# Attention with a quantised linear layer on one core: the prologue's products in another order, with half 1's queries last

## What is computed

```python
ct_q, ct_kv = x @ Wd_q + b, x @ Wd_kv + b            # 256 -> 128
query = (ct_q @ Wu_q + b) + rope(ct_q @ Wq_r + b)     # 128 -> 256
key   = (ct_kv @ Wu_k + b) + rope(x @ Wk_r + b)
value = ct_kv @ Wu_v + b
attn  = softmax(query_h @ key_h.T / sqrt(272))        # each head, 4096 x 4096
x = layernorm(x + concat_h(attn @ value_h) @ Wo + b)
x_int8 = clip(round(x / (max|x| / 127)), -128, 127)
x = layernorm(x + (x_int8 @ weight_int8.T) * x_scale * weight_scale.T + bias)
```

## Time and profile before

| | us |
|---|---|
| median of 3 runs | 1985.05 (1983.85 to 1987.11) |
| time of the profiled execution | 1983.67 |
| its span, first to last instruction | 1981.9 |
| ACT busy | 1815.3 (92% of the span) |
| PE busy | 1851.2 (93%) |
| DVE busy | 1582.6 (80%) |
| POOL busy | 163.4 (8%) |

### The profile page before, as it was taken

The page is one execution under the profiler, slowest core; times in us unless marked ns, Lnnn a source line. Parts: engine busy times, 40 slices in busy tenths (PEclk is TensorE's granted clock), DMA queues, the critical chain, the costliest instruction groups (busy, mean ns, idle before and its releaser), DMA issues.

```text
span 1981.9 us, 31796 instructions
## 1 busy us (share of the span) xinstructions
PE 1851.2 (93%) x13009; PEld 451.9 (23%) x13009; DVE 1582.6 (80%) x1500; ACT 1815.3 (92%) x2026; POOL 163.4 (8%) x134
## 2 busy tenths in 40 slices
PE   8967999999999999999999999999999999999955
PEld 3441112122121221221222222222122122222134
DVE  3653888888888888888888887888988898888458
ACT  4447999999999999999999999999999999999935
POOL 5723500000000000000000000000000300000012
PEclk9998999999999999999999999999999999999987
DMA  5644111101111111111121000111111101101012
GB/s 165 216 161 174 25 25 25 25 20 19 21 20 22 25 25 25 25 25 25 25 67 25 17 17 17 25 25 25 25 25 25 23 19 19 21 18 24 1 44 85
DMA packets 165483, 81.48 MB, mean 41 GB/s; under 512 B 130204, under 2 KB 146716, under 8 KB 164856
## 3 DMA queue, kind: packets, MB, share of 16 engines
q1 hardware_dynamic: 164024, 78.11, 15.3%
q10 hardware_dynamic: 1312, 1.32, 0.2%
HBM read 48.83 MB, written 29.23 MB: 39 GB/s over the span
## 4 chain that ended last, share of the span: by engine, by line
ACT 69%; PE 10%; issue 9%; DVE 6%; DMA 2%; POOL 2%; SPq 1%; ACTq 0%; DVEq 0%; POOLq 0%
ACT arena L800 55%; ACT parts_or_sums L800 14%; PE PS L601 5%; PE PS L558 3%; PE PS L640 1%; DVE arena L860 1%; PE PS L1044 1%; POOL arena L1363 1%; DVE bn L728 1%; DMA Qst<-parts_or_sums 1%; DMA arena<-arena 1%; POOL arena L1362 1%; DVE arena L1654 1%; POOL arena L1365 0%; DMA arena<-head_out 0%
## 5 line engine op out<-in xcount | busy, mean ns | idle before, releaser
L800 ACT ACTIVATE arena<-PS 128x1024 f32<-128x1024 f32 x1488 | 1396.5, 1134 | 31.4 <-PE PS L558 31.0
L601 PE MATMUL PS<-arena,Vh 128*32 128x512 f32 x6704 | 1082.6, 606 | 5.5 <-DVE arena L860 3.6
L558 PE MATMUL PS<-Qst,Kst 49*128 49x512 f16 x4096 | 710.7, 384 | 61.4 <-ACT arena L800 38.2
L860 DVE SCALAR_TENSOR_TENSOR arena<-arena 128x2048 f32<-128x2048 f32 x282 | 646.4, 2292 | 0.1
L836 DVE TENSOR_SCALAR arena<-PS 128x512 int32<-128x512 f32 x376 | 259.6, 690 | 269.4 <-PE PS L558 265.5
L558 PEld LDWEIGHTS PS<-Qst,Kst 49*128 49x128 f16 x4096 | 182.3, 93 | 1048.9 <-ACT arena L800 797.6
L601 PE MATMUL PS<-parts_or_sums,Vh 128*32 128x512 f32 x1488 | 386.0, 604 | 0.0
L800 ACT ACTIVATE parts_or_sums<-PS 128x1024 f32<-128x1024 f32 x372 | 369.3, 1137 | 2.8 <-PE PS L558 2.8
L601 PEld LDWEIGHTS PS<-arena,Vh 128*32 128x32 f32 x6704 | 155.9, 108 | 278.6 <-issue 270.0
L856 DVE SCALAR_TENSOR_TENSOR arena<-arena 128x2048 f32<-128x2048 f32 x94 | 216.0, 2297 | 0.0
L844 DVE TENSOR_SCALAR arena<-arena 128x2048 int32<-128x2048 int32 x94 | 115.7, 1230 | 7.3
(11 more groups left out here) (115 smaller groups left out, 606.6 us busy)
## 6 DMA issues: line engine op xcount, KB each, us to landing
Kst<-k_halves SPq DMA_DIRECT2D x64, 128.0 KB
Qst<-q_halves SPq DMA_DIRECT2D x64, 128.0 KB
Vh<-head_values SPq DMA_DIRECT2D x30, 256.0 KB, 4.4
arena<-xT_dram SPq DMA_DIRECT2D x8, 512.0 KB, 5.2
k_halves<-parts_or_sums SPq DMA_DIRECT2D x16, 256.0 KB, 2.4
k_whole<-arena SPq DMA_DIRECT2D x8, 512.0 KB, 3.3
q_halves<-parts_or_sums SPq DMA_DIRECT2D x16, 256.0 KB, 3.2
q_whole<-arena SPq DMA_DIRECT2D x8, 512.0 KB, 4.4
```

The lines of the kernel that those rows point to most:

```text
L558: return nc.tensor.matmul(out, Kst[par][low:low + HK + 1, at:at + 128], Qst[par][low:low + HK + 1, j * CH:(j + 1) * CH], start=True, stop= ...
L601: last = nc.tensor.matmul(bank(value_bank(t))[32 * j:32 * j + 32, :], Vh[t % 2][:, kt, :], moving, start=kt == first, stop=kt == last_kt)
L800: nc.scalar.activation(ring(at, k), bank(g % SLOTS * SLOT, k), ACT.Exp, scale=EXP_SCALE).then_inc(a.exp, 1)
L860: last = nc.vector.scalar_tensor_tensor(out=t, in0=t, scalar=POLY[3 - j], in1=power if j == 3 else mantissa, op0=ALU.add, op1=ALU.mult)
```

## The change

All products stand in one list, `PRODUCTS`, from which the programs of PE and ACT are written out without loops.

- Chunks 0 to 3 are made as before, keys and queries, eight products each. Then come the keys alone of chunks 4 to 7, then the queries alone of chunks 4 to 7, then the 16 groups of values. In the late parts the first product of chunk c+1 (`DKV` or `DQ_`) stands ahead of the last ones of chunk c.
- x and the tables of chunks 4 to 7 are loaded a second time for the late queries: `LOADS` has 12 entries, and a load's parity picks its buffer.
- DVE adds the two query weights of the upper 128 features once, so `QHI` is one matmul and not two: 13 per chunk and not 14. PE waits for this sum (`s_sum`).
- The lengths go into strips: each call writes four strips of 32 partitions of one bank, so that maxima and square roots read 128 partitions of 512 columns. The largest key length is brought to all partitions by a transpose and a matmul of one column. The calls stand between the late products.
- PE waits for the constants (`s_const`) ahead of its first product, where it waited after its last.
- On SP the stack of the first head (`load_stack`) stands between the loads of the late queries, the second stack after the stores of the last queries; shift rows come by way of DRAM.

```diff
+def make_products():
+    order = [("p", c, e) for c in range(HALF_CH) for e in range(8)]
+    late = range(HALF_CH, NCH)
+    order.append(("p", HALF_CH, DKV))
+    for c in late:
+        order += [("p", c, KR_)] + [("p", c + 1, DKV)] * (c + 1 < NCH) + [("p", c, UK_), ("p", c, KHI)]
+    order.append(("p", HALF_CH, DQ_))
+    for c in late:
+        order += [("p", c + 1, DQ_)] * (c + 1 < NCH) + [("p", c, QR_), ("p", c, UQ_), ("p", c, QHI)]
+    return order + [("v", 0, n) for n in range(KT // 2)]
...
+LOADS = list(range(NCH)) + list(range(HALF_CH, NCH))
...
+            def next_load(load, last_product, last_part):
+                if load + 2 < len(LOADS):
+                    sp.wait_ge(s_mm, DONE[last_product])
+                    load_x(LOADS[load + 2], load % 2)
+                    sp.wait_ge(s_rope, ROTATED[last_part])
+                    load_tables(LOADS[load + 2], load % 2)
...
+            for c in range(HALF_CH):
+                next_load(c, ("p", c, KHI), (c, "q"))
+                for n in "kq":
+                    store_parts(c, n)
+                    store_whole(c, n)
+            for c in range(HALF_CH, NCH):
+                next_load(c, ("p", c, KHI), (c, "k"))
+                store_parts(c, "k")
+                store_whole(c, "k")
+            next_load(NCH, ("p", HALF_CH, DQ_), (HALF_CH, "q"))
             for par in range(2):
-                load_stack(sp, fast.stack[par], par, par)
-            sp.wait_ge(s_shift, 1)
+                sp.wait_ge(s_parts["k"][par], 32 * HALF_CH)
+                sp.wait_ge(s_parts["q"][par], 32 * (HALF_CH // 2))
+            load_stack(sp, fast.stack[0], 0, 0)
+            next_load(NCH + 1, ("p", HALF_CH + 1, DQ_), (HALF_CH + 1, "q"))
+            for c in range(HALF_CH, NCH - 1):
+                store_parts(c, "q")
+                store_whole(c, "q")
+            store_shift(0)
+            store_parts(NCH - 1, "q")
+            store_whole(NCH - 1, "q")
+            sp.wait_ge(s_m, 16 * HALF_CH)
+            load_shift(sp, fast.stack[0], 0, 0)
+            load_stack(sp, fast.stack[1], 1, 1)
+            load_shift(sp, fast.stack[1], 1, 1)
+            store_shift(1)
...
-                    project(7, 7, [wcut(W_QR, lo=128), wcut(W_UQ, lo=128)], [cq, cq])
+                    QHI: ([wcut(W_UQ, lo=128)], [cq]),
...
             pe.wait_ge(s_const, 1)
-            pe.wait_ge(s_ev, E0 - 4)
+            for p in PRODUCTS:
+                if p == ("p", HALF_CH + 3, QR_):
+                    pe.wait_ge(s_ev, in_bank(SMALL_BANK))
+                    pe.wait_ge(s_kmax, 3)
+                    nc.tensor.transpose(PS[0:1, SMALL_BANK * CH:SMALL_BANK * CH + 128], kmax[:, 2:3], ident[:, :]).then_inc(s_kt, 1)
...
+                if p == ("v", 0, 13):
+                    lengths("q", 1, Q_LENGTH_BANKS[1])
+                product(p)
...
+            for p in PRODUCTS:
+                evacuate(p)
...
+                if p == ("v", 0, 2):
+                    shifts(0)
+                if p == ("v", 0, 14):
+                    shifts(1)
```

415 lines of the change are left out of this document (221 added, 194 removed).

## The result

| | before | after |
|---|---|---|
| median, us | 1985.31 (4 runs, 1983.85 to 1987.11) | 2007.03 (4 runs, 2006.57 to 2009.91) |
| ratio, 95% interval | | 1.0112 (1.0099 to 1.0125) |
| profiled execution: time, span | 1983.67, 1981.9 | 2009.91, 2008.1 |
| first exponential | 157.56 | 181.12 |

The change makes the kernel 1.1% slower. Slower was the forecast; the size was not: 1989 with a range to 1997, against 2007. The first exponential came 23.6 us later than before, where I had counted 3.9.

The account below looks back on a forecast made before the run. ACT's exponentials set the pace, so only the prologue's end could move: first exponential 157.6 to 161.5 (+3.9), −0.5 for the clock, +3.4 on 1983.67 gives 1987.1; 1988.5 from the median, 1989 with hand-overs; range 1977 to 1997, likeliest case 1984 to 1993.

Parts of the forecast that it names:

- Steps 1 and 2: PE's start waits for constants, +7.3 us; summed query weights save 0.86 us per chunk, half 0 done at 60.8.
- Steps 3 and 4: Late keys: x loads wait behind SP's stores and two buffers; chunk 5 gap 6.4 us, chunks 6 and 7 2 to 4 each.
- Step 5: Late queries: x of chunk 7 asked for at 128.3 behind eight stack DMAs, lands at 133; PE idle 8 us.
- rival B: Slower still: clock falls in every x wait (+5), chunk 7's x lands behind the whole stack (+3); 1996 us, chance 0.23.
- Step 6: Values on PE: 14.4 us, 15.4 with lengths; largest-key-length wait costs nothing; first exponential at 161.5.
- Steps 7 and 8: Shift rows land about 159.5 and cannot set the start unless slipping by 2; other edits save nothing on the deciding path.
- the −0.5 us: Attention's start: PE may enter with the full clock after the values, −1.5 to 0 us, taken as −0.5.
- Its rule on the clock: PE's matmul bursts between DMA waits start slow each time; holding for all six x waits costs 1.7 us for three more.
- C: Faster rival: x loads land in 3.7 us everywhere and PE's clock stays up; −9, 1977 us, chance 0.21.
- D: Rival that PE works nearly without gaps, needing a third x buffer; start about 130, −27, 1958 us, chance 0.04.
- E: Rival that SP's first shift row slips behind stores by 2 to 6 us; 1991 to 1995 us, chance 0.07.

Follow-up runs that it names:

- e1: Changed kernel with PE's wait for the constants moved from its first product to its first call of lengths; median 1999.93 us, ratio 1.0069.
- e5: Kernel before, with only the wait for the constants put ahead of PE's first product; median 1991.65 us, ratio 1.0034.
- e4: Changed kernel with late products in plain order, nothing of chunk c+1 ahead of chunk c; median 1988.60 us, ratio 1.0013.
- f1: Changed kernel with the first stack's eight DMAs moved on SP to just ahead of the store of chunk 6's queries; median 1994.95 us, ratio 1.0047.
- h1: Changed kernel with each two-part stack DMA issued as two of one part; median 2002.34 us, ratio 1.0075.
- f4: Changed kernel with x of chunks 4 to 7 loaded once and kept, tables of chunks 6 and 7 in the second stack's space; 1979.17 us, ratio 0.9966.
- h2: Kernel before with each two-part stack DMA issued as two of one part; median 1978.13 us, ratio 0.9960.
- f3: Changed kernel with late constants' wait, plain order of late products and first stack's DMAs just ahead of chunk 6's query store; 1976.99 us, ratio 0.9951.
- g1: Changed kernel with late x kept, constants and first stack later, chunk 3's x before chunk 0's stores, late query wholes stored earlier; 1972.11 us, ratio 0.9936.
- e2: Changed kernel with SP's load of x and tables for chunk 7's queries ahead of the first stack's loads; median 2008.04 us, ratio 1.0114.

## Why the prediction had the sign right and the size wrong

- *Steps 1 and 2 held.* PE's first product at 13.71 (14.3 forecast), half 0 done by 60.4 (60.8). That this start costs about 7 us is shown on both sides by the times: e1 takes it away from after (7.1 by the medians), e5 adds it to before (6.8 by the ratio, 8.8 in the trace). That all of it travels down the chain of loads, as I had it, is not shown: in e1 only 3.3 us of it are left at the last load of x.
- *Steps 3 and 4 held, each a little short.* x of chunk 5 came at 75.10 (72.2), `KHI` of 4 to 7 ended at 82.3, 92.1, 103.9 and 109.8 (79.1, 91.9, 101.9, 108.0). The waits that I derived from two buffers of x are all there, and e4 shows what the order ahead costs by itself: 19.6 us (18.4 by the medians), though 16.9 of the 32.4 us of waits for x stay without it.
- *Step 5 failed: the load of x for chunk 7's queries.* I had it asked for at 128.3 and wrote "with the stack's bytes ahead of it I let it land at 133", a landing of 4.7 us. It was asked for at 133.02 and PE went on at 144.39. The first part, +4.7, is 1.8 from step 4, 0.7 from x of chunk 5's landing, and 2.5 from a swap that stood beside the load of x for chunk 6: 5.1 us from its issue to POOL's start, where I had 2.6 from the earlier trace rows; the stack's issue was 0.5 shorter. The second part is the mistake, +6.7: I priced the eight stack DMAs by the time in which SP issues them and added almost nothing for the transfers behind it. f1 (4.05 us with the stack out of the way), h1 (4.2 us with the stack's DMAs cut) and the packets of after show that the load waited behind transfers on two engines. The 13.38 us of the earlier trace rows, a row of 4 KB behind 16 stack DMAs, eight of them of two parts, was the row to price it by; I had put that down to the values. The bound on this term, for which I wrote +3 in rival B, was too tight.
- *Then PE, +1.6.* From x's landing to the last product, 10.2 us against 8.6: mostly the slow clock, 1.7 of which I had counted.
- *Step 6 failed too.* I wrote that the wait for the largest key length "costs nothing by this count". It was over at 163.4 and PE stood still for 2.71 us; the 20 records behind it took 7.63 us, where 12 took 2.86 at the end, so 20 would take 4.8. That is 5.6 of the 5.7 us by which the last value was late. The wait was late because DVE's four steps for chunk 6's queries took 6.2 us beside POOL's rotation of chunk 7 (157.12 to 163.3), where I had priced them alone, 3 us. The row with DVE's price beside POOL stood in the earlier trace rows.
- *The end.* Last value to first exponential 4.4 us, 3.5 counted. Sum of the misses: 4.7 + 6.7 + 1.6 + 5.7 + 0.9 = 19.6, which is 181.1 − 161.5.
- *Steps 7 and 8 held in their result,* though step 7 gave the wrong reason for the 13.38 us. The shift rows were issued at 168.96, the first scores waited for PE and POOL, and the exponentials show no new wait. The second stack's rows are issued by 175.4. The clock was down again at the attention's start (0.50 from 178 to 181), so the −0.5 us for it did not come.
- *The rivals.* B (slower still, 1996) was nearest, and I had both its mechanisms but not their size. Its rule on the clock held for four of six waits for x: after 5.67, 2.44, 4.09 and 14.55 us the records ran slow (the window from 75 at a clock of 0.53, mostly the lower level, 1.2 GHz), after 2.67 and 2.97 they did not (1.00 from 86.7). The rule of the Trainium skill, "TensorE: Matmul & The Clock Gate", section "HAM oscillation — how this bites in real kernels", so describes most of these bursts, and not all. C is out: landings were 4 to 6 us, not 3.7. D, as the lists promise, fails for a second reason: f4 has all of x early, more than the third buffer I named, and still starts at 150.3, not 130, because the buffers that ACT writes wait for DVE and for stores. Of that I had seen nothing. E did not decide.

The change is no better on the cut stacks: h1 against h2 is 24.2 us, after against before 21.7.

What stays open: how the 12 us between 161.56 (e4) and 149.56 (f3) split between constants and stack, since edits overlap (by the medians 7.1, 18.4 and 12.1 us alone make 37.6, together they make 30.0); when PE's clock falls, which moved 3 to 4 us between kernels that differ in something else; and the 7 us spread behind the first exponential. That DVE and POOL are the last bound of the prologue is read from waits in f4 and g1; no run made them faster.

## What to carry to other kernels

A product pulled ahead of its turn moves the release of a buffer back, and with two buffers the next load starts only then: count from the last reader of the buffer to the load, not from the first product that needs it. Price a load by what stands ahead of it on its queue until that has been moved, not until it has been issued; where a transfer is slow at a low DMA share, look at its shape first and cut it so that all engines take part. When one such wait is closed, look for the next one in the same trace: in e2, f3, f4 and g1 the time came back as a wait on another buffer.

## What the runs showed that I had not expected

- A load of 512 KB behind eight stack DMAs let PE go on 11.0 to 12.2 us after its issue in four kernels, against 4.05 without them (f1) and 4.2 behind twelve DMAs with the same rows in another cut (h1). In before the cut is worth 13.6 us of the first exponential, of which about 2.4 are the clock's, and 9.3 us of the median.
- Behind the same DMAs the issue itself slows: a pair of stores took SP 5.05 us (e2), the pair just ahead of it in the queue 0.93.
- Eight matmuls of lengths in strips of 32 partitions took 0.61 to 0.62 us of PE's time, against 1.89 onto 16 partitions; I had taken 1.
- PE's clock after a wait of 2.4 to 3.0 us goes both ways: slow after 2.44, and at 164.74 after 2.71 (0.57); full after 2.67 and 2.97, as before after 2.78 and 2.68. Longer waits differ too: slow after 3.17 in before, full after 3.15 in e1 (1.00 from 111.67) and 3.23 in e5 (1.00 from 105.51).
